# Projecting queries and keys first, values beside the first score maxima, and scoring one tile in 384 + 256 keys

## What is computed

```python
def attention_fwd(x, wq, wk, wv, wo, n_heads=32):
    xq = (x @ wq.T).reshape(B, T, n_heads, hd)
    xk = (x @ wk.T).reshape(B, T, n_heads, hd)
    xv = (x @ wv.T).reshape(B, T, n_heads, hd)
    xq = rotary_pos_emb(xq)
    xk = rotary_pos_emb(xk)
    scores = jnp.einsum('bqhd,bkhd->bhqk', xq, xk) * scale
    scores = jnp.where(causal[None, None], scores, NEG_INF)
    ...
    scores = jnp.einsum('bkgqd,bksd->bkgqs', qg, k) / math.sqrt(HD)
    bias = jnp.where(rel > 0, NEG_INF, slopes[:, :, None, None] * rel)
    attn = jax.nn.softmax(scores + bias[None], axis=-1)
```

## Time and profile before

| what | us |
|---|---|
| median of 3 runs (1667.99 to 1669.5) | 1669.45 |
| the profiled execution, whole | 1668.87 |
| its span, first to last instruction | 1666.8 |
| TensorE busy | 1535.4 |
| VectorE busy | 1132.0 |
| ScalarE busy | 827.7 |

### The profile page before, as it was taken

How to read it: one execution, slowest core, us unless ns; L and a number is a source line. 1 busy time by engine, 2 the same in 40 slices (tenths; PEclk the granted TensorE clock), 3 DMA queues, 4 the chain that set the end, 5 groups by cost and what they waited for, 6 DMA issues and landing times. The chain is left out here.

```text
span 1666.8 us, 25633 instructions
## 1 busy us (share of the span) xinstructions
PE 1535.4 (92%) x9096; PEld 1186.6 (71%) x9096; DVE 1132.0 (68%) x2845; ACT 827.7 (50%) x2104; POOL 392.8 (24%) x356
## 2 busy tenths in 40 slices
PE   2895999999798799999999999999999999999969
PEld 2772444444487688888888888888888888888757
DVE  6546777774376577677677677677767767767745
ACT  2451455656433455555555555556455555555521
POOL 4100100001253231322323133133133133131130
PEclk9996899999999899999999999999999999999979
DMA  3143533321110100100100010010010010000011
GB/s 144 36 117 90 72 43 40 40 39 53 38 33 1 38 24 4 39 10 17 33 7 26 1 39 26 1 39 26 1 38 26 1 39 17 10 1 1 1 45 52
DMA packets 42656, 54.56 MB, mean 33 GB/s; under 512 B 6304, under 2 KB 24992, under 8 KB 42528
## 3 DMA queue, kind: packets, MB, share of 16 engines
q1 hardware_dynamic: 41568, 52.52, 12.7%
q10 hardware_dynamic: 960, 0.39, 0.1%
HBM read 44.31 MB, written 8.39 MB: 32 GB/s over the span
## 5 line engine op out<-in xcount | busy, mean ns | idle before, releaser
L1653 ACT ACTIVATE prob<-prob,ab_neg_max 128x128 f32<-128x128 f32 (+7 forms) x256 | 201.5, 787 | 252.5 <-DVE ab_neg_max L1760 251.5
L1777 DVE TENSOR_TENSOR ab_pt_l<-ps,ab_pt_h 128x512 fp32r<-128x512 f32 x288 | 197.8, 687 | 73.8 <-ACT ab_pt_h L1681 72.9
L1681 ACT CAST ab_pt_h<-ps 128x512 fp32r<-128x512 f32 x288 | 171.5, 597 | 111.9 <-PE ps L1566 111.2
L1760 DVE CUSTOM_DVE_ANT_0 prob<-ps,rel 128x512 f32<-128x512 f32 (+3 forms) x256 | 150.3, 587 | 107.1 <-PE ps L52 106.4
L989 DVE TENSOR_REDUCE ra_part_max<-ps 128x1 f32<-128x128 f32 (+1 forms) x336 | 164.8, 550 | 50.3 <-PE ps L889 32.6
L50 PE MATMUL ps<-ab_w_h,ab_xt_h 128*128 128x512 f32 (+1 forms) x512 | 186.5, 364 | 6.8 <-DVE ab_v_l L1797 6.3
L1566 PE MATMUL ps<-ident,prob 128*128 128x128 f32 x1152 | 173.5, 273 | 5.8 <-DVE ab_qt_l L1769 4.5
L52 PE MATMUL ps<-ab_w_h,ab_xt_l 128*128 128x512 f32 (+1 forms) x512 | 174.1, 340 | 0.0
L51 PE MATMUL ps<-ab_w_l,ab_xt_h 128*128 128x512 f32 (+1 forms) x512 | 173.6, 339 | 0.0
L1785 DVE TENSOR_SCALAR prob<-prob,ab_recip 128x128 f32<-128x128 f32 (+7 forms) x256 | 166.5, 650 | 9.1
L1566 PEld LDWEIGHTS ps<-ident,prob 128*128 128x128 f32 x1152 | 138.1, 140 | 27.4 <-DVE ab_qt_l L1769 5.8
(11 more groups left out here) (252 smaller groups left out, 3499.7 us busy)
## 6 DMA issues: line engine op xcount, KB each, us to landing
f_raw<-in_wqkv SPq DMA_DIRECT2D x32, 384.0 KB, 3.7
f_raw<-in_wbo SPq DMA_DIRECT2D x32, 256.0 KB, 2.6
ra_first_rows<-in_wa SPq DMA_DIRECT2D x4, 768.0 KB, 9.7
parts<-pa_stage SPq DMA_DIRECT2D x12, 256.0 KB, 3.4
parts<-f_raw SPq DMA_DIRECT2D x12, 256.0 KB, 3.2
ra_q_st<-parts SPq DMA_DIRECT2D x24, 128.0 KB, 6.0
ra_k_st<-parts SPq DMA_DIRECT2D x24, 128.0 KB, 6.3
ra_first_rows<-parts SPq DMA_DIRECT2D x24, 128.0 KB, 6.2
```

Source lines behind the costliest of these rows:

```text
L1653: act.activation(prob[:, t % 2, h, 0:w], prob[:, t % 2, h, 0:w], ACT.Exp, bias=neg_max[:, t % 2, h, pieces_per_head(t % NT) - 1:pieces_per ...
L1681: act.copy(pt_h[:, n % PT, :], ring_bank("p", u, j)).then_inc(pt_high, 1)
L1760: dve.tensor_tensor_reduce(out=prob[:, t % 2, h, k0:k1], in0=ps[:, n % 2, a:b], in1=const["rel"][:, SLIDE - i * P + k0:SLIDE - i * P + k1] ...
L1777: dve.tensor_tensor(pt_l[:, n % PT, :], ring_bank("p", u, j), pt_h[:, n % PT, :].bitcast(F32), ALU.subtract).then_inc(emptied, 1)
```

## The change

Three things change.

1. The projection runs in two. `project` makes queries and keys alone, 24 matmuls for a tile; `project_values` makes the values, 12 matmuls for a tile, and stands behind the last tile and between the pieces of the first maxima. The raw weights come in eight pieces, four of 1024 columns and then four of 512, whose loads share one semaphore.
2. TensorE transposes `rot` as f32, 8 transposes for a tile, and the three bf16 parts are made from the transposed tile: ScalarE writes the high part from PSUM (`high`), VectorE subtracts it (`split`), ScalarE makes the middle part (`mid`) and VectorE the low one. The parts are written straight to `stage`, and SyncE stores each part when it is made.
3. In the stream `score_spans` takes the place of `key_spans`. It differs for tile 4 alone: 384 + 256 keys, where there were 512 + 128.

```diff
-    BANKS = (0, 1, 2, 3, 4, 5)
+    BANKS = (2, 3, 4, 5, 6, 7)
...
         def _(sp):
             for h in range(NT // 2):
-                sp.wait_ge(staged_dve, 2 * (h + 1))
-                sp.wait_ge(staged_act, 4 * (h + 1))
                 for a in range(3):
+                    sp.wait_ge((high_done, mid_done, low_done)[a], 4 * (h + 1))
...
             def project(i):
-                    for n in range(3):
+                    for n in range(2):
...
+            def project_values(i):
+                if i >= 2:
+                    pe.wait_ge(v_done, i - 1)
+                cols = slice(i * P, (i + 1) * P)
+                for k in range(KC):
+                    last = three_pass(pe, ps[:, i % 2, :], (xt_h[:, k, cols], xt_l[:, k, cols]),
+                                      (w_h[:, k, 2 * C:], w_l[:, k, 2 * C:]), k == 0, k == KC - 1)
+                last.then_inc(v_projected, 1)
...
             def turn(i):
-                pe.wait_ge(low_done, i + 1)
+                pe.wait_ge(rot_done, i + 1)
+                for n in range(2):
+                    if i >= 2:
+                        pe.wait_ge(rest_done, 2 * (i - 2) + n + 1)
+                    for m in range(KC):
+                        last = pe.transpose(turn_bank(i, n)[:, m * P:(m + 1) * P],
+                                            rot[:, i % 2, (n * KC + m) * P:(n * KC + m + 1) * P], const["ident"][:, :])
+                    last.then_inc(transposed, 1)
...
-            pe.wait_ge(rot_done, NT)
-            pe.wait_ge(v_done, NT)
-            first.score_pieces(pe)
+            pe.wait_ge(weights.w_low, 2 * KC)
+            pe.wait_ge(rot_done, NT)
+            project_values(0)
+            turn(NT - 1)
+            project_values(1)
+            pe.wait_ge(rest_done, 2 * NT)
+            for h in range(NT // 2):
+                first.score_pieces(pe, h)
+                for i in ((2, 3), (4, 5), (6, 7), ())[h]:
+                    project_values(i)
             first.turn_max(pe)
...
         def _(act):
+            def high(i):
+                stage_free(act, i)
+                for n in range(2):
+                    act.wait_ge(transposed, 2 * i + n + 1)
+                    act.copy(staged(i, n, 0), by_rows(turn_bank(i, n))).then_inc(high_done, 1)
+            def mid(i):
+                for n in range(2):
+                    act.wait_ge(rest_done, 2 * i + n + 1)
+                    act.copy(staged(i, n, 1), by_rows(rest[:, i % 2, n, :])).then_inc(mid_done, 1)
+            def take_values(i):
+                act.wait_ge(v_projected, i + 1)
+                act.copy(v_all[:, i, :], ps[:, i % 2, :]).then_inc(v_done, 1)
...
-                if i < 2:
+                if i < 6:
                     weights.split_high(act, 2 + i, 3 + i)
...
+            take_values(0)
+            high(NT - 1)
+            mid(NT - 1)
+            take_values(1)
             act.wait_ge(stored[1], 16 * 6 * (NT // 4))
             first.load_rows(act, 0, NT // 2 - 1, (1,))
             first.load_rows(act, 1, NT // 2 - 1, (1,))
+            for i in range(2, NT):
+                take_values(i)
...
+            def split(i):
+                stage_free(dve, i)
+                for n in range(2):
+                    dve.wait_ge(high_done, 2 * i + n + 1)
+                    dve.tensor_tensor(by_rows(rest[:, i % 2, n, :]), by_rows(turn_bank(i, n)), staged(i, n, 0),
+                                      ALU.subtract).then_inc(rest_done, 1)
+                for n in range(2):
+                    dve.wait_ge(mid_done, 2 * i + n + 1)
+                    dve.tensor_tensor(staged(i, n, 2), by_rows(rest[:, i % 2, n, :]), staged(i, n, 1),
+                                      ALU.subtract).then_inc(low_done, 1)
...
+def score_spans(i):
+    w = P * (i + 1)
+    at = min(w, W if w - W != P else W - P)
+    return [(0, at)] + ([(at, w)] if w > at else [])
...
-                k0, k1 = key_spans(i)[c]
+                k0, k1 = score_spans(i)[c]
```

More of the change, by code:

```diff
@@ L75, with __init__ @@
 class Weights:
-    def __init__(self, nc, ctx, own, tag, pieces, apart=False, raw=None, raw_in=None):
+    def __init__(self, nc, ctx, own, tag, pieces, apart=False, raw=None, raw_in=None, raw_full=None):
         self.pieces = pieces
+        self.raw_full = raw_full or [16] * len(pieces)
         self.apart = apart
@@ L452, in raw_weights @@
         flat = self.rows[:, :, :].rearrange("p b n -> p (b n)").bitcast(F32)
-        return [flat[:, k * 3 * C:(k + 1) * 3 * C] for k in range(KC)]
+        return [flat[:, k * 3 * C:k * 3 * C + 2 * C] for k in range(KC)] + [flat[:, k * 3 * C + 2 * C:(k + 1) * 3 * C] for k in range(KC)]
     def load_rows(self, queue, b, h, sides=(0, 1)):
@@ L544, in rotary_projection_block @@
         rot = o_all[:, NT // 2:NT, :].rearrange("p (b r) c -> p b (r c)", b=2)
-        part = spare[:, 0:3 * 2 * C].bitcast(BF16).rearrange("p (b a n) -> p b a n", b=2, a=3)
+        rest = spare[:, 0:2 * 2 * W].rearrange("p (b n t) -> p b n t", b=2, n=2)
         stage = [half.rearrange("p (a m t) -> p a m t", a=3, t=2 * P)
@@ L622, in project @@
                 last.then_inc(projected, 1)
-            def turn(i):
-                pe.wait_ge(low_done, i + 1)
[L626 to L635, removed]
+            def project_values(i):
[6 more added lines that the diff above has]
+                last.then_inc(v_projected, 1)
+            def turn(i):
+                pe.wait_ge(rot_done, i + 1)
[5 more added lines that the diff above has]
+                                            rot[:, i % 2, (n * KC + m) * P:(n * KC + m + 1) * P], const["ident"][:, :])
                     last.then_inc(transposed, 1)
             norm.turn(pe, 0)
-            for i in range(NT + 1):
-                if i < NT:
-                    project(i)
+            for i in range(NT):
+                project(i)
                 if i >= 1:
                     turn(i - 1)
+            pe.wait_ge(weights.w_low, 2 * KC)
             pe.wait_ge(rot_done, NT)
-            pe.wait_ge(v_done, NT)
-            first.score_pieces(pe)
+            project_values(0)
[6 more added lines that the diff above has]
+                    project_values(i)
             first.turn_max(pe)
@@ L660, in _ @@
                 for n in range(2):
-                    odd = ps[:, 3 * (i % 2) + n, :].rearrange("p (m two) -> p m two", two=2)[:, :, 1]
+                    odd = ps[:, 2 * (i % 2) + n, :].rearrange("p (m two) -> p m two", two=2)[:, :, 1]
                     for f in range(2):
@@ L666, in _ @@
                 last.then_inc(prod_done, 1)
[L667 to L671, removed]
-                if i >= 1:
[L673 to L679, removed]
+                if i >= 1:
+                    high(i - 1)
+                    mid(i - 1)
+            take_values(0)
+            high(NT - 1)
+            mid(NT - 1)
+            take_values(1)
             act.wait_ge(stored[1], 16 * 6 * (NT // 4))
@@ L703, in _ @@
                 last.then_inc(rot_done, 1)
-                dve.wait_ge(high_done, i + 1)
-                dve.tensor_tensor(rot[:, i % 2, :], rot[:, i % 2, :], part[:, i % 2, 0, :],
-                                  ALU.subtract).then_inc(rest1_done, 1)
-                dve.wait_ge(mid_done, i + 1)
-                dve.tensor_tensor(part[:, i % 2, 2, :], rot[:, i % 2, :], part[:, i % 2, 1, :],
-                                  ALU.subtract).then_inc(low_done, 1)
-            take_part(dve, dve.tensor_copy, staged_dve, NT - 1, 0)
+                if i >= 1:
+                    split(i - 1)
+            split(NT - 1)
             first.max_of_pieces(dve)
@@ L1950, in hybrid_layer_kernel @@
                     w_h, w_l = [own.enter_context(nc.sbuf_tensor(f"a_w_{part}", [P, KC, 3 * C], F32R)) for part in "hl"]
-                    pieces = [(ins["wa"][k * P:(k + 1) * P, :], w_h[:, k, :], w_l[:, k, :]) for k in range(KC)]
-                    weights = Weights(nc, ctx, own, "a", pieces, apart=True, raw=first.raw_weights())
+                    pieces = [(ins["wa"][k * P:(k + 1) * P, cols], w_h[:, k, cols], w_l[:, k, cols])
+                              for cols in (slice(0, 2 * C), slice(2 * C, 3 * C)) for k in range(KC)]
+                    raw_in = [ctx.enter_context(nc.semaphore(f"a_raw_in{k}")) for k in range(KC + 1)]
+                    weights = Weights(nc, ctx, own, "a", pieces, apart=True, raw=first.raw_weights(),
+                                      raw_in=raw_in + raw_in[KC:] * (KC - 1), raw_full=[16] * KC + [16 * KC] * KC)
                     norm = LayerNorm(nc, ctx, own, "an", x, xt_h, xt_l, const, ps, banks=(6, 7),
```

43 lines of the change are left out of this document (21 added, 22 removed).

## The result

The changed kernel takes 1659.00 us in the median of 4 runs (1656.44 to 1659.23), against 1668.72 us (1667.08 to 1669.5, 4 runs) before: ratio 0.9943, 95% interval 0.9928 to 0.9958. It is faster by 9.7 us, inside the range forecast. The profiled execution took 1659.02 us with a span of 1657.1 us, 9.7 less than before. Of these 9.7 us of span, 3.1 come by the end of the first projection, 5.2 in the stream's eight groups and 0.9 in the stream's last output projection; the remaining 0.5 lie in the stages between. The forecast had 9.6, 5.3 and nothing.

The account below looks back on a forecast made before the run. TensorE was taken to bound the first seven projection tiles and the stream, SyncE's stores and row loads the projection's end. 1668.87 - 9.6 (projection's end) - 5.3 (spans) = 1654.0, forecast 1654.5 us as the median; range 1647 to 1664.

Parts of the forecast that it names:

- some 20 us, released by a value copy: End of projection: TensorE stands idle until about 122 us, because ScalarE's value copies queue behind its 12 row loads.
- first rival: End of projection: values fill the wait, only the chain of row loads counts; maxima 27.6 us earlier, 1636.5 us; chance 0.04.
- The gain there: End of projection: the last 16 maxima start at 139.5 instead of 149.17 us, a gain of 9.6 us.
- The first normalised tile is released at 19.6: Start: shorter weight pieces release it at 19.6 instead of about 20.8 us; the second tile starts at 38.
- T + 65.5: SyncE's chain: last stores landed 65.5 us after the third tile's end T, 49.95 us; two more pairs at 18.1 each.
- The sum of 18.4 us: From ScalarE free at 121.1 to the last maxima: 0.7 + 7.3 + 4.3 + 5.5 + 0.6 us, including 1.8 for low clock.
- the clock stays at 1.2 GHz through the burst: Rival, end of projection: 48 value matmuls at half speed cost 9.2 us beyond the 1.8 counted; 1663.5 us; chance 0.08.
- 6.45 us for a tile: Projection tiles: 24 matmuls, 5.5 us, and 8 f32 transposes, 0.95 us, on TensorE, instead of 10.2 us.
- the alternative of 6 us later: Start: the last three normalisations each held 3.2 us beside GpSimd; second tile 6 us later, 1660.5 us; no chance given.
- The spans: Stream, tile 4: 384 + 256 saves 0.055 us in each of 96 matmuls, 5.3 us in all.
- The rival that they save nothing: Stream: the shorter spans save nothing, since scores hand two banks to and fro with VectorE; 1660 us; chance 0.07.

Follow-up runs that it names:

- both repairs: Changed kernel with value copies 1 to 5 ahead of ScalarE's store wait and the four value weight pieces loaded in the projection block: 1635.71 us.
- the projection alone: Changed kernel with the old `key_spans` kept in the stream: 1664.61 us, ratio 0.9982 to before.
- the late weights: Changed kernel with SyncE loading the four value weight pieces at the head of the projection's block, not in the block ahead: 1656.58 us.
- Filling the wait: Changed kernel with 76 added matmuls, results unused, on TensorE between the second pair's last maximum and values 4: 1654.49 us.
- the last kernel: Changed kernel, value weights loaded in the projection block, second group's row loads behind the last pair's, value copies 1 to 3 ahead of ScalarE's wait: 1632.14 us.
- the second group's rows last: Changed kernel, value weights loaded in the projection block, SyncE loading the second group's rows behind the last pair's, only value copy 1 ahead: 1635.01 us.
- three copies ahead: Changed kernel with value copies 1 to 3, instead of copy 1 alone, ahead of ScalarE's wait for the last stores: 1646.77 us.

## Why the prediction came out right, and where it was wrong

**The mechanism at the end of the projection: right.** The prediction let TensorE stand behind ScalarE's 12 loads for "some 20 us, released by a value copy"; it stood 21.23, released by `v_all` of L679. Its first rival, that the values fill the wait, was put at 1636.5 us; with the copies moved ahead the kernel takes 1638.2. That rival was a correct picture of another order.

**The gain there: mis-sized, 3.1 us instead of 9.6.** Three terms make the 6.6 us by which the last maxima are late (146.08 against 139.5):

- *The start, 1.6 us.* "The first normalised tile is released at 19.6" left out that the change issues four more DMAs in the block ahead. It was 22.10. The DMAs of the row transfers had all been counted, those of the weights not. Loading them later gave back 1.3 us by itself and 2.0 in the kernel with both repairs.
- *SyncE's chain, 2.0 us.* T + 65.5 was forecast from the third tile's end at T. With 1.6 us from the start the last loads should begin at 117.1; they began at 119.08. The third landing of 4.24 us for 2.8 is 1.4 of it. The loads of the first two pairs took 11.99 and 11.43 us instead of 11.1, 1.2 more, and the first stores had landed 0.7 us sooner than forecast.
- *What follows the copy, 3.0 us.* The sum of 18.4 us from ScalarE's release was 21.4. The low clock was taken as 1.8 us from 28.77 in the trace of before; after 21 us without work it held for 5.7 us, 2.8 us of loss, and a second low stretch, which the sum did not have, cost 1.4 us. The pieces took 0.7 us more than 4.3. In the profile of the projection alone the same term is 143.97 - 124.41 = 19.6 and in that of the late weights 142.46 - 123.50 = 19.0, so 0.6 to 1.2 us of this miss stand in all three profiles and the rest changes with the clock. Filling the wait showed the clock's whole part, 4.4 us, of which the sum had counted 1.8.

The rival "the clock stays at 1.2 GHz through the burst" was true in part: of the 48 value matmuls 13 were slow behind the restart and 6 in values 6. That is 2.4 us beyond the 1.8 counted, where the rival had 9.2.

**The tiles: right.** 6.45 us for a tile was forecast; turns follow each other by 6.42 (77.32 and 83.74), and a turn is 0.8 to the next matmul where 0.95 was taken. The first tiles, with the shorter way from a tile to its parts, brought SyncE's chain forward: its first stores came at 54.42 us for 77.21, 22.8 earlier, while the second tile was 11.1 earlier. The later tiles brought it nothing more, since SyncE's period of 18.4 to 19.7 us for a pair stood above the 12.8 of two tiles, until the second group's loads were taken out of it.

**Normalisations beside GpSimd: right.** The last three take 0.91 to 1.64 us, none 3.2; the alternative of 6 us later did not come. Where one still falls beside a memset it is held as before: the mask's `tensor_scalar` took 2.95 us at 39.51, to the end of GpSimd's first memset at 42.4, and 0.19 in the trace of before. The Trainium skill (SBUF — State Buffer, "Who interferes with whom") has the later of two such instructions wait for the whole of the other; the trace agrees.

**The spans: right,** 0.65 us a group forecast as 0.66. The rival that they save nothing fell with the run of the spans alone, 5.0 us.

**The sum** was 4.5 us below the median: 6.5 us too much gain at the first place and 0.1 at the spans, less the 0.9 of the last output projection, 0.5 of the other stages, 0.15 outside the span and 0.5, because the profiled execution stood at the median and not below it. The range held because it had room for a weaker start and a lower clock, both of which came in part. That the 0.9 us made up for some of the miss was luck: no term of the sum had it.

## What to carry to other kernels

Before moving an engine's copies behind its DMA issues, write down whose bank each copy frees: a copy of 0.6 us, placed behind 5.6 us of loads which themselves wait for stores, held another engine for 21 us, and moving four of them was worth twice the whole change. Count the DMAs that a change adds ahead of a block's end, at about 0.5 us each, and price any long wait of TensorE with what its clock costs afterwards, as a range. Where a queue paces a chain by its number of issues, those that nobody waits for yet can go to its end, but the gain ends where the next engine's work does.

## What the runs showed of the hardware

- How long TensorE stays at 1.2 GHz behind one and the same wait (21.2 to 22.3 us) differs: 13 value matmuls (5.7 us) in after, 11 (4.9 us) in the projection alone, 8 (3.6 us) with the late weights. The Trainium skill (TensorE: Matmul & The Clock Gate, "What's actually happening") says that it is "run-variable"; these traces agree, in three kernels with the same order there, and the last maxima came up to 2.4 us apart by it. Four runs of after, at 1659.02, 1659.23, 1658.98 and 1656.44 us, have a mean granted clock of 0.973, 0.973, 0.973 and 0.975.
- The clock fell also behind 3 us in which TensorE was two thirds busy (108 to 111 us in the last kernel, and the same in that with both repairs), and did not in the same place of the kernel with the second group's rows last (1.99 of 3.0 us busy, 110.5 to 113.5).
- Ahead of the first value tile TensorE waits 2.57 us in every kernel of this order. Behind it the clock was at 1.2 GHz for over 3 us in five of the nine kernels, from the first matmul (after, at 87.34 us) or up to four matmuls later, and in the four others (the projection alone, both repairs, and the last two) it stayed at 2.4 GHz.
- Six stores of 256 KB mostly landed 2.8 us behind their last issue. But for the third pair, landing between 95 and 102 us, it was 3.7 to 4.4 us in six of the kernels and 2.9 in the one that differs from after only by three copies ahead; where the last pair fell into that time it was 3.3 and 4.5. Why is open; no run was made for it.
